# Attention scores in 16 array tiles of 32x32, the second token tile reversed, a new order of all calls

## The chip, the cores and the metric

The kernel runs on one core of a Trainium2 chip. A core has five engines with queues of their own: TensorE (PE) for matrix products, VectorE (DVE), ScalarE (ACT), GpSimd (POOL), and SyncE (SP), which issues most DMAs. They meet only through semaphores. The time is that of one execution on the device in microseconds; lower is better. Everything is fp32 but two mask constants.

## The reference, cut to what matters

For 8 batches of 256 tokens of 128 features, with xn = layernorm(x), the kernel adds three things: x, a one-head attention block with an output norm (a0/h0 in the names), and a transformer block with 16 heads of 8 features and causal attention, followed by a gated sum over four small expert networks. The part that the change touches:

```python
h = _rms(x, n1_w)
heads = lambda w_: (h @ w_.T).reshape(B, T, HEADS, HD).transpose(0, 2, 1, 3)
q = _rms(heads(wq), qn_w); k = _rms(heads(wk), kn_w); v = heads(wv)
scores = jnp.einsum('bhqd,bhkd->bhqk', q, k) * HD ** (-0.5)
scores = jnp.where(causal[None, None], scores, -jnp.inf)
attn = jax.nn.softmax(scores, axis=-1)
ao = jnp.einsum('bhqk,bhkd->bhqd', attn, v)...@ wo.T
```

The experts are: e0 = gelu, down; e1 = silu gate, product, down; e2 = four layers with three gelus (l1, l2, l3, down); e3 = two gelus (in, up, down). The gate is a softmax over four logits of which the two largest are kept.

## The kernel before, in words

A batch is two token tiles of 128 (j for queries, kt for keys). Every engine has a hand-written list of small functions, called with the batch number (`batches()` on PE and VectorE, straight lists on GpSimd and ScalarE); the order of the calls is the schedule, and work of several batches is interleaved in it. PSUM is eight banks: four hold one group of scores (`scores_ps`), the other four (a, b, even, odd) are handed from use to use by `claim`, which waits until the reader of the last use is done.

The heads are taken in 4 groups (g) of 4 lanes. A lane is a strip of 32 rows of the PE array: `qT` has the transposed queries of all heads, `kT[:, g]` the keys in which all features but those of the group's heads are zero, so that 32 rows of both, multiplied, give one head's scores. `scores(n, g)` (L229) puts keys on the partitions and queries on the columns: for key tile 0 all 256 queries, for key tile 1 the last 128 only, since earlier queries don't see them. That is 2 x 4 products, each in an array tile of 32 rows x 128 columns (L246). `exp_group` (L724) takes the exponential of all 4 x 384 columns at once, `mask` (L563) on GpSimd zeroes the later keys in the two diagonal 128x128 squares of each lane with one select, `weigh_v` (L271, L275) multiplies by the values and, through a column of ones in `v_aug`, sums the weights; VectorE transposes and divides (`pv_turn`, `heads_inverse`, `heads_divide`, `ao_turn`), PE projects (`wo_project`), and the residual, its norm and the transposed `xfT` feed the experts (`up_layer` L333, `square_layer` L360, `e3_up_layer` L376, `down` L392).

Ahead of the scores stand, for each batch: `ln_statistics` (VectorE), `ln_variance`, `ln_pow` (GpSimd), `ln_normalise`, `x_turn` (PE transposes xn, L186), `qkv_project` (L216), `qkv_copy` (ScalarE), `qk_square` to `qk_norm` on VectorE (a reciprocal root by a guess and corrections), `qk_turn` (PE, L186), `q_copy` and `k_copy` (ScalarE). `fold_weights` multiplies two weight matrices once.

The softmax takes no maximum if a bound on the weights allows it. VectorE computes that flag at run time (`bound_scores`), each of PE and VectorE reads it and takes one of two branches. With the inputs used here the branch without maximum runs (`searching = False`).

Of the kernel before, what the change touches and what calls it, by code (L numbers as in the profile page):

```python
# [4 lines left out]
ALU = mybir.AluOpType  # L5
# [6 lines left out]
P = 128  # L12
# [18 lines left out]
def fused_block(nc: bass.Bass, x, cols, rows, w_proj, w_first, w_up, w_mid, w_down, out):  # L31
# [5 lines left out]
    TILES = SEQ // P  # L37
# [9 lines left out]
    with ExitStack() as ctx:  # L47
# [9 lines left out]
        def sem(name):  # L57
# [30 lines left out]
        minus_half = sb("minus_half", [P, TILES])  # L88
        lower = sb("lower", [P, EXPERTS, EXPERTS])
# [50 lines left out]
        names = """ident_ready lower_ready lanes_ready cols_in rows_in flags_in proj_in first_in up_in mid_in down_in  # L140
                   proj_scaled m0_full m0_ready vfc_full vfc_ready flag_ready k_rows_ready zeros_ready masks_ready
# [28 lines left out]
        def _(pe):  # L170
# [58 lines left out]
            def scores(n, g):  # L229
# [10 lines left out]
                if n == 0 and g == 0:  # L240
                    pe.wait_ge(s["vfc_ready"], 1)
                for kt in range(TILES):
                    for lane in range(LANES):
                        rows = slice(32 * lane, 32 * lane + 32)
                        ps = scores_ps[:, lane, 0:SEQ] if kt == 0 else scores_ps[:, lane, SEQ:SEQ + P]
                        ins = T.matmul(ps, kT[p][rows, g, kt * P:(kt + 1) * P], qT[p][rows, kt * P:SEQ],  # L246
                                       start=kt == 0, stop=kt == 1 and not searching, tile_position=(32 * lane, 0))
                if searching:
# [6 lines left out]
                    for lane in range(LANES):  # L255
                        own = scores_ps[:, lane, :].rearrange("p (n q) -> p n q", q=SEQ)[:, :, 0:P]
                        ins = T.matmul(own, ident_bf[:], later_keys[:].unsqueeze(1).to_broadcast([P, TILES, P]),
                                       start=False, stop=True)
# [138 lines left out]
            def find_maxima(n):  # L397
# [11 lines left out]
                for r, (j, kt) in enumerate(ROUND_LIST):  # L409
# [8 lines left out]
                    if kt == j:  # L418
                        for lane in range(LANES):
                            ins = T.matmul(scores_ps[:, lane, :].rearrange("p (g k) -> p g k", k=P), ident_bf[:],  # L420
                                           later_keys_q[:].unsqueeze(1).to_broadcast([P, GROUPS, P]), start=False,
                                           stop=True)
# [8 lines left out]
            def batches():  # L431
                x_turn(0); qkv_project(0, 0); fold_weights(); q0_project(0); qkv_project(0, 1); a0_scores(0, 0)
                a0_scores(0, 1); x_turn(1); qk_turn(0); q0_project(1); find_maxima(0); scores(0, 0); x_turn(2)
                qkv_project(1, 0); scores(0, 1); qkv_project(1, 1); fc_row(0); scores(0, 2); a0_scores(1, 0)
                weigh_v(0, 0); weigh_v(0, 1); scores(0, 3); a0_scores(1, 1); weigh_v(0, 2); x_turn(3); weigh_v(0, 3)
                fc_row(1); qk_turn(1); q0_project(2); find_maxima(1); scores(1, 0); wo_project(0); qkv_project(2, 0)
                a0_scores(2, 0); scores(1, 1); qkv_project(2, 1); a0_scores(2, 1); scores(1, 2); weigh_v(1, 0)
                xf_turn(0); weigh_v(1, 1); scores(1, 3); gate(0); l1_layer(0); e3_in(0); weigh_v(1, 2); x_turn(4)
                weigh_v(1, 3); e1_first(0); e3_up_layer(0); qk_turn(2); wo_project(1); l2_layer(0); e0_up(0)
                fc_row(2); find_maxima(2); scores(2, 0); l3_layer(0); e1_second(0); xf_turn(1); qkv_project(3, 0)  # L440
                scores(2, 1); e3_in(1); gate(1); down(0, 0); down(0, 1); q0_project(3); scores(2, 2)
                qkv_project(3, 1); e3_up_layer(1); l1_layer(1); scores(2, 3); weigh_v(2, 0); weigh_v(2, 1)
                l2_layer(1); e0_up(1); weigh_v(2, 2); weigh_v(2, 3); e1_first(1); qk_turn(3); e1_second(1)
                wo_project(2); find_maxima(3); scores(3, 0); l3_layer(1); a0_scores(3, 0); qkv_project(4, 0)
                scores(3, 1); xf_turn(2); qkv_project(4, 1); down(1, 0); gate(2); down(1, 1); x_turn(5); scores(3, 2)
                e1_first(2); e0_up(2); scores(3, 3); weigh_v(3, 0); l1_layer(2); e1_second(2); q0_project(4)
                weigh_v(3, 1); e3_in(2); a0_scores(3, 1); weigh_v(3, 2); weigh_v(3, 3); l2_layer(2); e3_up_layer(2)
                wo_project(3); qk_turn(4); fc_row(3); l3_layer(2); a0_scores(4, 0); find_maxima(4); scores(4, 0)
                qkv_project(5, 0); down(2, 0); down(2, 1); xf_turn(3); qkv_project(5, 1); scores(4, 1); l1_layer(3)
                e0_up(3); gate(3); scores(4, 2); weigh_v(4, 0); l2_layer(3); e3_in(3); a0_scores(4, 1); weigh_v(4, 1)  # L450
                scores(4, 3); weigh_v(4, 2); l3_layer(3); e3_up_layer(3); fc_row(4); weigh_v(4, 3); x_turn(6)
# [945 lines left out]
```

## Time and profile before

| what | us |
|---|---|
| median of 3 runs | 233.01 (232.93 to 233.16) |
| profiled execution | 233.21 |
| its span in the profile | 231.5 |
| PE busy | 199.3 |
| ScalarE busy | 170.2 |
| VectorE busy | 153.4 |
| GpSimd busy | 107.7 |

The busy times are unions of an engine's instructions over the span. PE's instructions overlap each other, and the ends of its instructions are modelled by the profiler; the distance between two starts is the surer measure. `PEld` is PE's loading of the fixed operand, which runs beside the products. The granted clock is the share of PE's full 2.4 GHz that the chip let through: 1.00 or 0.50.

### The profile page before, as it was taken

The numbers are of one execution on the slowest core, as the hardware profiler recorded it, in microseconds if no ns is written. First come the engines' busy times: TensorE is split into PE (matmuls) and PEld (weight loads), VectorE is DVE, ScalarE is ACT, GpSimd is POOL, SyncE is SP. The second block draws the span as 40 slices with busy tenths as digits, with TensorE's granted clock in tenths as the row PEclk, the third lists the DMA queues.
The fourth block names the chain that finished last, engine by engine and source line by source line (L and its number), as shares of the span: only waits on it lengthen the run. The fifth ranks groups of instructions, "written<-read, shape, count | busy, mean of one in ns | idle before, by whom it ended". The sixth has DMA issues, their size and how long they took to land. (4 is left out here: it accounts for less than half of the span.)

```text
span 231.5 us, 5985 instructions
## 1 busy us (share of the span) xinstructions
PE 199.3 (86%) x2132; PEld 145.4 (63%) x2132; DVE 153.4 (66%) x534; ACT 170.2 (74%) x288; POOL 107.7 (47%) x190
## 2 busy tenths in 40 slices
PE   0557765989999998898999899999999999969892
PEld 0325433656868765765777678667786786747682
DVE  6453489279837881597669486797479847843354
ACT  2225843778998989997989998899999677636610
POOL 6851587865381715251476266515622536720000
PEclk9985999599999999999999999999999999999999
DMA  5930000000000000000000000000000000000001
GB/s 130 385 97 1 4 0 0 3 1 3 0 1 3 25 0 0 3 25 1 1 3 27 0 0 3 27 0 4 0 25 0 4 0 25 3 0 0 1 3 52
DMA packets 5393, 5.00 MB, mean 22 GB/s; under 512 B 498, under 2 KB 4850, under 8 KB 5362
## 3 DMA queue, kind: packets, MB, share of 16 engines
q1 hardware_dynamic: 5072, 4.39, 5.8%
q8 instruction: 19, 0.31, 0.5%
q10 hardware_dynamic: 290, 0.20, 0.4%
q14 instruction: 12, 0.10, 0.1%
HBM read 3.54 MB, written 1.05 MB: 20 GB/s over the span
## 5 line engine op out<-in xcount | busy, mean ns | idle before, releaser
L563 POOL TENSOR_SCALAR_AFFINE_SELECT probs<-probs 128x1024 f32<-128x1024 f32 x32 | 35.3, 1102 | 49.2 <-ACT probs L724 48.9
L724 ACT ACTIVATE probs<-scores_ps 128x1536 f32<-128x1536 f32 x32 | 46.4, 1449 | 6.9 <-PE scores_ps L246 6.6
L246 PEld LDWEIGHTS scores_ps<-qT,kT 32*128 32x128 f32 x512 | 24.8, 195 | 15.4 <-issue 11.8
L246 PE MATMUL scores_ps<-qT,kT 32*128 32x128 f32 (+1 forms) x512 | 31.7, 363 | 3.1 <-ACT probs L724 3.0
L360 PE MATMUL even_ps<-l_h,mid 128*128 128x256 f32 x128 | 31.8, 391 | 1.1 <-DVE e_s L1029 1.1
L360 PEld LDWEIGHTS even_ps<-l_h,mid 128*128 128x128 f32 x128 | 23.0, 189 | 6.8 <-DVE e_s L1029 1.7
L778 ACT ACT_TABLE_LOAD x18 | 23.1, 1283 | 2.3 <-PE even_ps L360 1.8
L333 PE MATMUL odd_ps<-xfT,up 128*128 128x256 f32 x80 | 21.8, 387 | 0.2 <-DVE e_h L1040 0.2
L271 PE MATMUL a_ps<-probs,v_aug 128*32 128x256 f32 x256 | 20.3, 389 | 1.5 <-DVE pv_rows L1048 1.4
L778 ACT ACTIVATE l_h<-even_ps 128x512 f32<-128x512 f32 x24 | 14.4, 599 | 8.7 <-PE even_ps L360 6.8
L1235 DVE SCALAR_TENSOR_TENSOR acc<-even_ps,wts,acc 128x96 f32<-128x96 f32 x32 | 10.2, 318 | 14.2 <-PE even_ps L392 11.7
L333 PE MATMUL even_ps<-xfT,up 128*128 128x256 f32 x64 | 17.8, 400 | 0.4 <-DVE e_s L1029 0.2
L333 PEld LDWEIGHTS odd_ps<-xfT,up 128*128 128x128 f32 x80 | 14.5, 190 | 3.1 <-DVE e_h L1040 0.8
L216 PE MATMUL a_ps<-qkvT,xnT 128*128 128x384 f32 x32 | 15.2, 558 | 0.6 <-ACT xnT L742 0.6
L284 PE MATMUL b_ps<-xnT,q0T 128*128 128x256 f32 x32 | 11.2, 435 | 4.0 <-ACT a_exp L731 4.0
L731 ACT ACTIVATE a_exp<-b_ps,a_negmax 128x256 f32<-128x256 f32 x16 | 7.5, 472 | 9.1 <-DVE a_negmax L1122 9.1
L830 ACT ACTIVATE kT<-a_ps,k_rows 128x256 f32<-128x256 f32 x32 | 13.7, 493 | 0.0
L186 PE MATMUL b_ps<-ident,xn 128*128 128x128 f32 x16 | 4.0, 336 | 11.0 <-DVE xn L1222 8.1
L333 PEld LDWEIGHTS even_ps<-xfT,up 128*128 128x128 f32 x64 | 11.0, 189 | 3.4 <-ACT l_h L778 1.3
L724 ACT ACT_TABLE_LOAD x10 | 12.8, 1283 | 0.2
L275 PE MATMUL a_ps<-probs,v_aug 128*32 128x128 f32 x256 | 12.9, 273 | 0.0
L1048 DVE STREAM_TRANSPOSE pv_rows<-a_ps 128x512 f32<-128x512 f32 x16 | 11.3, 704 | 1.8 <-PE a_ps L275 1.8
(149 smaller groups left out, 433.3 us busy)
## 6 DMA issues: line engine op xcount, KB each, us to landing
x_sb<-in_x SPq DMA_DIRECT2D x8, 128.0 KB, 6.5
out<-acc SPq DMA_DIRECT2D x8, 128.0 KB, 1.8
mid<-in_mid SPq DMA_DIRECT2D x1, 640.0 KB, 7.4
up<-in_up SPq DMA_DIRECT2D x1, 578.0 KB, 6.3
downs<-in_down SPq DMA_DIRECT2D x1, 512.0 KB, 8.2
first<-in_first SPq DMA_DIRECT2D x1, 320.0 KB, 5.6
proj<-in_proj SPq DMA_DIRECT2D x1, 192.0 KB, 2.9
row<-in_rows ACTq DMA_DIRECT2D x1, 192.0 KB, 4.8
```

The lines of the kernel that those rows point to most:

```text
L216: T.matmul(ps[:, 0:3 * D], xnT[n % X_COPIES][:, j * P:(j + 1) * P], qkvT[:], start=True, stop=True).then_inc(full_sem(fill), 1)
L246: ins = T.matmul(ps, kT[p][rows, g, kt * P:(kt + 1) * P], qT[p][rows, kt * P:SEQ], start=kt == 0, stop=kt == 1 and not searching, tile_pos ...
L271: T.matmul(rows, v_aug[p][:, 0, GROUPS * lane + g, :], probs[g][:, lane, 0:SEQ], start=True, stop=False, tile_position=(0, 32 * lane))
L275: ins = T.matmul(rows[:, P:SEQ], v_aug[p][:, 1, GROUPS * lane + g, :], probs[g][:, lane, SEQ:SEQ + P], start=False, stop=True, tile_positi ...
L284: T.matmul(ps, q0T[n % Q0_COPIES][:, j * P:(j + 1) * P], xnT[n % X_COPIES][:], start=True, stop=True).then_inc(full_sem(fill), 1)
L333: ins = T.matmul(ps[:, m * SEQ:(m + 1) * SEQ], wT[:, m * P:(m + 1) * P], xfT[n % XF_COPIES][:], start=True, stop=True)
L360: ins = T.matmul(ps[:, m * SEQ:(m + 1) * SEQ], wT[:, at_col:at_col + P], src[:, ci, :], start=(ci == 0), stop=(ci == HC - 1))
L563: nc.gpsimd.affine_select(out=own, in_=own, compare_op=ALU.is_ge, fill=0.0, base=0, pattern=[[0, LANES * TILES], [1, P]], channel_multipli ...
L724: nc.scalar.activation(probs[g][:, :, 0:SEQ + P], scores_ps[:, :, 0:SEQ + P], ACT.Exp).then_inc(s["exp_done"], 1)
L778: nc.scalar.activation(dst[n % 2][:].rearrange("p c q -> p (c q)"), ps_of(fill), ACT.Gelu).then_inc(read_sem(fill), 1)
L830: nc.scalar.activation(kT[n % HEAD_COPIES][:, g, :], ps_of("QKT")[:, SEQ:2 * SEQ], ACT.Copy, scale=k_rows[:, g:g + 1]).then_inc(s["k_copie ...
L1048: V.transpose(pv_rows[n % 2][:, 2 * pair:2 * pair + 2].rearrange("p g n e -> p (g n e)"), ps_of(fill)).then_inc(read_sem(fill), 1)
```

## The change

- `scores`: all groups but the first of batch 0 are now 32 products in array tiles of 32 rows x 32 columns: for each key tile, 4 blocks of 32 keys x 4 lanes. A block of key tile 0 takes only the queries from its own first key on (256, 224, 192, 160 columns).
- The second token tile is stored in reverse, on the host, on the way in and out. In it a block of keys c is seen by the first 32c + 32 stored queries (32, 64, 96, 128 columns). What the skipped places of PSUM hold from before goes through the exponential and is zeroed by the mask.
- `mask`: two selects of 128x512, one for each token tile, with opposite comparisons, in place of one of 128x1024.
- The branch with a maximum keeps whole products and gets a second mask constant.
- `v_aug` is filled with ones by ScalarE (three `fill_heads`) in place of three pairs of memsets on VectorE.
- `keep_busy(count)`: products of a zeroed tile into the bank "odd" that nobody reads, 3 ahead of the flag's read and 10 in the first calls of batch 0.
- The rows' constants (bias, gamma, beta) are loaded by SP's queue after x(2), not by ScalarE's; x(4) is loaded ahead of `mid`.
- All four lists of calls are new.

```diff
+            def keep_busy(count):
+                for _ in range(count):
+                    T.matmul(banks["odd"][:, 0:SEQ], spare[:, 0:P], spare[:], start=True, stop=True)
...
+                whole = searching or (n == 0 and g == 0)
                 for kt in range(TILES):
-                    for lane in range(LANES):
-                        rows = slice(32 * lane, 32 * lane + 32)
-                        ps = scores_ps[:, lane, 0:SEQ] if kt == 0 else scores_ps[:, lane, SEQ:SEQ + P]
-                        ins = T.matmul(ps, kT[p][rows, g, kt * P:(kt + 1) * P], qT[p][rows, kt * P:SEQ],
-                                       start=kt == 0, stop=kt == 1 and not searching, tile_position=(32 * lane, 0))
+                    if whole:
...
+                        continue
+                    for c in range(P // 32):
+                        keys = slice(kt * P + 32 * c, kt * P + 32 * c + 32)
+                        at_col, seen = (32 * c, slice(32 * c, SEQ)) if kt == 0 else (SEQ, slice(P, P + 32 * c + 32))
+                        for lane in range(LANES):
+                            rows = slice(32 * lane, 32 * lane + 32)
+                            ins = T.matmul(scores_ps[32 * c:32 * c + 32, lane, at_col:at_col + seen.stop - seen.start],
+                                           kT[p][rows, g, keys], qT[p][rows, seen], start=kt == 0, stop=kt == 1,
+                                           tile_position=(32 * lane, 32 * c))
...
             def mask(n, g):
                 pool.wait_ge(s["exp_done"], GROUPS * n + g + 1)
-                own = probs[g][:].rearrange("p l (n q) -> p (l n) q", q=SEQ)[:, :, 0:P]
-                nc.gpsimd.affine_select(out=own, in_=own, compare_op=ALU.is_ge, fill=0.0, base=0,
-                                        pattern=[[0, LANES * TILES], [1, P]], channel_multiplier=-1
-                                        ).then_inc(s["masked"], 1)
+                for kt, sign in enumerate((1, -1)):
+                    own = probs[g][:, :, kt * SEQ:kt * SEQ + P]
+                    ins = nc.gpsimd.affine_select(out=own, in_=own, compare_op=ALU.is_ge, fill=0.0, base=0,
+                                                  pattern=[[0, LANES], [sign, P]], channel_multiplier=-sign)
+                ins.then_inc(s["masked"], 1)
...
+            def fill_heads(p):
+                if p == 0:
+                    act.wait_ge(s["halves_ready"], 1)
+                nc.scalar.activation(v_aug[p][:].rearrange("p j h e -> p (j h e)"),
+                                     minus_half[:, 0:1].to_broadcast([P, TILES * HEADS * 32]), ACT.Copy, scale=-2.0
+                                     ).then_inc(s["heads_filled"], 1)
```

The first calls of PE's new list, and its last (before, the first scores had two of batch 1's calls ahead of them, `x_turn(1)` and `q0_project(1)`, and the list ended in `down(6, 0); down(6, 1); down(7, 0); down(7, 1)`):

```diff
+                keep_busy(4); fold_weights(); x_turn(0); keep_busy(1); qkv_project(0, 0); x_turn(1); qkv_project(0, 1)
+                q0_project(0); qkv_project(1, 0); a0_scores(0, 0); qkv_project(1, 1); keep_busy(3); x_turn(2)
+                keep_busy(1); q0_project(1); qkv_project(2, 0); a0_scores(0, 1); qk_turn(0); fc_row(0); find_maxima(0)
+                scores(0, 0); a0_scores(1, 0); qkv_project(2, 1); scores(0, 1); a0_scores(1, 1); qk_turn(1)
+                scores(0, 2); x_turn(3); keep_busy(1); scores(0, 3); weigh_v(0, 0); weigh_v(0, 1); fc_row(1)
...
+                xf_turn(7); l3_layer(6); e3_in(7); gate(7); down(6, 0); down(6, 1); a0_scores(7, 1); e1_first(7)
+                e3_up_layer(7); fc_row(7); l1_layer(7); e1_second(7); l2_layer(7); e0_up(7); l3_layer(7); down(7, 0)
+                down(7, 1)
```

## Rows read from the trace of the kernel before

**Rows 1.** The page, busy time, share and instructions of TensorE

```profile
PE 199.3 (86%) x2132; PEld 145.4 (63%) x2132; DVE 153.4 (66%) x534; ACT 170.2 (74%) x288; POOL 107.7 (47%) x190
```

**Rows 2.** Windows: stretch, its length, busy us of each engine, clock, DMA

```profile
core 0: us, PE busy (x) PEld busy (x) DVE busy (x) ACT busy (x) POOL busy (x), PEclk, DMA share, GB/s
15.60:22.40 6.80, 4.50 (x18) 2.69 (x22) 3.82 (x19) 2.78 (x10) 2.15 (x6) 0.50 0.00 1
30.90:39.50 8.60, 4.06 (x47) 2.35 (x44) 8.46 (x24) 3.03 (x8) 7.17 (x12) 1.00 0.00 0
39.50:46.30 6.80, 6.76 (x42) 4.09 (x45) 2.68 (x10) 5.30 (x14) 5.16 (x9) 0.50 0.01 2
60.00:180.00 120.00, 115.65 (x1292) 86.34 (x1294) 85.48 (x304) 110.78 (x177) 56.23 (x87) 1.00 0.03 7
200.00:220.00 20.00, 16.54 (x90) 12.40 (x82) 9.48 (x35) 10.28 (x21) 3.22 (x6) 1.00 0.00 0
```

**Rows 3.** Timeline of PE, one group cut at 120.30, then whole: start, us, what

```profile
120.26 0.50 PE L246 MATMUL scores_ps<-qT,kT 32*128 32x256 f32 x4
...
120.26 0.94 PE L246 MATMUL scores_ps<-qT,kT 32*128 32x256 f32 x16
121.12 1.13 PE L333 MATMUL even_ps<-xfT,up 128*128 128x256 f32 x4
```

**Rows 4.** Timeline of PE, the gate's small products

```profile
123.05 0.40 PE L321 MATMUL b_ps<-up,xfT 128*64 128x4 f32 x8
```

**Rows 5.** Timeline of PE, values in four tiles of 32 columns

```profile
124.24 0.64 PE L271 MATMUL a_ps<-probs,v_aug 128*32 128x256 f32 x8
```

**Rows 6.** Timeline of the first 11 us, several engines; in brackets idle before, releaser

```profile
4.87 0.14 DVE L913 TENSOR_SCALAR bounded<-widest 1x1 int32<-1x1 f32 x1
5.87 0.19 POOL L648 TENSOR_SCALAR ln_tmp<-ln_mv 128x2 f32<-128x2 f32 x1 [0.40 <-DVE ln_mv L1215]
7.55 0.69 PE L186 MATMUL b_ps<-ident,xn 128*128 128x128 f32 x2 [7.55 <-DVE xn L1222]
8.80 1.65 PE L216 MATMUL a_ps<-qkvT,xnT 128*128 128x384 f32 x2 [0.56 <-ACT xnT L742]
10.24 0.63 PE L191 MATMUL scores_ps<-first 128*128 128x128 f32 x2
```

**Rows 7.** Timeline from 19 to 41 us, PE and VectorE

```profile
19.53 1.09 PE L186 MATMUL a_ps<-ident,qk_n 128*128 128x128 f32 x4
21.46 1.40 PE L246 MATMUL scores_ps<-qT,kT 32*128 32x256 f32 x16
26.56 0.61 DVE L1140 SCALAR_TENSOR_TENSOR h<-b_ps,a_row,xn_b 128x128 f32<-128x128 f32 x2 [6.90 <-PE b_ps L293]
38.72 0.66 PE L186 MATMUL a_ps<-ident,qk_n 128*128 128x128 f32 x4 [1.66 <-DVE pv_rows L1048]
40.21 1.67 PE L246 MATMUL scores_ps<-qT,kT 32*128 32x256 f32 x16
```

**Rows 8.** Timeline of ScalarE, an exponential, a tanh, a table load

```profile
214.11 0.21 ACT L774 ACTIVATE gate_b<-gate_a 128x8 f32<-128x8 f32 x1
214.23 0.58 ACT L767 ACTIVATE e_t<-even_ps 128x512 f32<-128x512 f32 x1
214.82 1.28 ACT L778 ACT_TABLE_LOAD   x1
```

**Rows 9.** Groups of GpSimd by line: count, busy us, mean ns, idle before

```profile
L563 POOL TENSOR_SCALAR_AFFINE_SELECT probs<-probs 128x1024 f32<-128x1024 f32 x32 | 35.3, 1102 | 49.2 <-ACT probs L724 48.9
L529 POOL TENSOR_SCALAR_AFFINE_SELECT ident<-ident 128x128 f32<-128x128 f32 x1 | 0.3, 298 | 0.2 <-POOL ident L528 0.2
```

**Rows 10.** Timeline of PE at the end

```profile
218.41 1.96 PE L360 MATMUL even_ps<-l_h,mid 128*128 128x256 f32 x8
220.21 1.03 PE L333 MATMUL odd_ps<-xfT,up 128*128 128x256 f32 x4
221.17 0.88 PE L392 MATMUL even_ps<-downs,e_h 128*64 128x96 f32 x16
224.26 0.88 PE L392 MATMUL even_ps<-downs,e_h 128*64 128x96 f32 x16 [0.23 <-DVE acc L1235]
```

More of the change, by code:

```diff
@@ L431, in batches @@
             def batches():
[L432 to L451, printed above, removed]
@@ new lines, in batches @@
+                scores(1, 1); wo_project(0); qkv_project(3, 1); a0_scores(2, 0); scores(1, 2); weigh_v(1, 0)
+                weigh_v(1, 1); a0_scores(2, 1); scores(1, 3); xf_turn(0); weigh_v(1, 2); l1_layer(0); gate(0)
+                e3_in(0); x_turn(4); weigh_v(1, 3); l2_layer(0); qk_turn(2); e3_up_layer(0); wo_project(1)
+                e1_first(0); e0_up(0); fc_row(2); find_maxima(2); scores(2, 0); e1_second(0); l3_layer(0); xf_turn(1)
+                qk_turn(3); scores(2, 1); gate(1); e3_in(1); q0_project(3); down(0, 0); down(0, 1); scores(2, 2)
@@ new lines, in batches @@
+                qkv_project(4, 1); x_turn(5); l3_layer(2); wo_project(3); e3_up_layer(2); qkv_project(5, 0)
+                q0_project(4); down(2, 0); xf_turn(3); qkv_project(5, 1); e3_in(3); l1_layer(3); e0_up(3); l2_layer(3)
+                gate(3); down(2, 1); a0_scores(4, 0); e1_first(3); qk_turn(4); e1_second(3); x_turn(6); find_maxima(4)
+                scores(4, 0); e3_up_layer(3); l3_layer(3); scores(4, 1); qk_turn(5); down(3, 0); down(3, 1)
+                scores(4, 2); weigh_v(4, 0); weigh_v(4, 1); scores(4, 3); a0_scores(4, 1); weigh_v(4, 2); fc_row(4)
@@ new lines, in batches @@
+                weigh_v(4, 3); find_maxima(5); scores(5, 0); q0_project(5); qkv_project(6, 0); scores(5, 1)
+                wo_project(4); qkv_project(6, 1); a0_scores(5, 0); scores(5, 2); weigh_v(5, 0); a0_scores(5, 1)
+                scores(5, 3); xf_turn(4); weigh_v(5, 1); e3_in(4); l1_layer(4); gate(4); weigh_v(5, 2); fc_row(5)
+                e0_up(4); l2_layer(4); x_turn(7); weigh_v(5, 3); e3_up_layer(4); qk_turn(6); l3_layer(4)
+                find_maxima(6); scores(6, 0); wo_project(5); e1_first(4); e1_second(4); q0_project(6)
@@ L468, in _ @@
+            keep_busy(3)
             pe.wait_ge(s["flag_ready"], 1)
@@ L706, in _ @@
+            h0_add(7); x1_add(7)
         @block.scalar
@@ L1341, in _ @@
+                down(7, 1, 2); down(7, 1, 3)
+            V.memset(spare[:], 0.0).then_inc(s["spare_ready"], 1)
             bound_scores()
```

321 lines of the change are left out of this document (161 added, 160 removed).

## Prediction, made before the change ran

> **What bounds the kernel now.** I read the page's shares first: TensorE (PE) leads with 86% of the span [rows 1]. A share is an average over stages, so next comes the table of windows [rows 2]. From 60 to 180 us PE is busy for 115.65 of 120 us and ScalarE for 110.78: there PE sets the pace with ScalarE close behind, and a us taken from PE alone is worth nearly a us only as long as ScalarE follows. The same table shows two stretches of 6.8 us, 15.6 to 22.4 and 39.5 to 46.3, in which the granted clock was 0.50 (1.2 of 2.4 GHz). The second was full of work, 6.76 us of it. Ahead of it, from 30.9 to 39.5, PE had 4.06 us of work in 8.6 us. So PE was starved, fell to half clock, and then paid double for its work. The sum is made against the profiled execution, 233.21 us with a span of 231.5; the median of the runs is 233.01, so what holds for the one holds for the other within 0.2.
>
> **Scores in 16 tiles.** One group of scores (L246) is 8 products, 16 matrix instructions: an fp32 product takes two. What it costs is not the 0.94 of its row but the distance to the next start, 120.26 to 121.12, 0.86 us [rows 3]. The price of a column: eight instructions of 256 columns (L360) from 218.41 to the next product at 220.21, 1.80 us [rows 10], 0.225 each, 0.88 ns a column. Each lane streams 256 + 128 = 384 columns twice: 0.675 us. The other 0.185 is the first weight load and the switch to other products. That lanes overlap is in the rows: four instructions have begun in the first 0.05 us, and sixteen one after the other would take over 2 us [rows 3]. Now each of 16 tiles streams 288 columns (256+32, 224+64, 192+96, 160+128): 2 x 288 x 0.88 = 0.507. If all sixteen overlap as the four do, a group is 0.507 + 0.185, and 0.05 for twelve more starts at the rate of those four: 0.74 us. 31 groups change (the first stays whole): 31 x 0.12 = -3.7. Bounds: 0.65 from below (no stagger, a shorter weight load), -6.5; from above the nearest row of small products is L321, eight instructions of 4 columns in 0.40, 0.05 us each [rows 4]; 64 such are 3.2 us, +73 in all. I stay near the scores' own row: L321 has two tiles at a time, while the four starts within 0.05 us show that the stream of instructions is faster.
>
> **The clock and the hole before it.** The new order projects batch 1 ahead of the first scores and puts qk_turn(1) before scores(0, 2). Before, qk_turn(1) was the product at 38.72 that waited for VectorE, busy 8.46 of those 8.6 us, and scores(1, 0) could only follow at 40.21 [rows 2, 7]. VectorE had stood idle for 6.9 us until 26.56 [rows 7]; its work for batch 1 can go there. Of 4.5 us of idle PE I take 3.0 as filled (bounds 0 and 4.5). With that the fall of the clock at 39.5 has lost its cause: half of 6.76, -3.4 (bounds 0 and -3.4).
>
> **The head.** Idle products (two instructions of 256 columns, 0.45 us at full clock, twice that at half) raise the clock earlier. Batch 0's chain had at half clock a transpose of 0.69, a projection of 1.65, four transposes of 1.09 and the first scores, 1.40 [rows 6, 7], 4.83 together. The scores' row is 0.94 at full clock, a third less [rows 3]; a third to a half of 4.83 is 1.6 to 2.4: -2.0. The weight products and what they wait for (10.24 until the next projection step, 1.1) leave the middle of the chain: -1.1. Against it x_turn(0) now stands behind four idle products, which start when the flag is there (4.87 + 0.14) and last 3.6 at half clock, and behind four short weight instructions: about 9.2 instead of 7.55, +1.6. Net -1.5, bounds +2 and -3. The memsets leave VectorE, but GpSimd took up batch 0's variance at 5.87 after only 0.40 of waiting [rows 6], its constants stay ahead of it, so at most 0.4 comes of that, counted as nothing; on ScalarE the three fills (1024 elements, 1.1 us each by the 0.58 for 512 [rows 8]) lie before its first copy, which waits for the product at 7.55. Should the fills last until 9 they would delay it by what is over. The shift of the rows' DMA to SP's queue puts it behind three loads and puts x(3) and the three large weight loads behind it; its reader (biased) is not on batch 0's chain: nothing. If it is late, h0_variance and masks behind it on GpSimd's queue are late too.
>
> **ScalarE.** Its list of functions changes kind (exponential against gelu) 34 times instead of 38, if tanh costs no switch on either side. The rows show that: tanh at 214.23 stands right behind an exponential at 214.11 with no load between, and the load comes for the gelu behind it [rows 8]. A load is 1.28 us: -5.1 of ScalarE's work. In 60 to 180 PE idles only 4.35 us, so a quarter of it, -1.3, is taken (0 to -3).
>
> **The masks.** One select over 1024 elements is 1.10 us, one over 128 is 0.30 [rows 9]. On that line 512 cost 0.64, two 1.29: +0.19 a group, +6 for GpSimd, which has room. On the path only in the last batch: +0.2.
>
> **The tail.** Before, four down calls stood at the end, batch 6's from 221.17, batch 7's from 224.26 [rows 10]. Now the two of batch 6 go before batch 7's expert layers, into 3.46 us of idle PE between 200 and 220 [rows 2]: -3.1. Late next is the last gelu (0.58 for 512 elements by tanh's row [rows 8]), once covered by e1_second at 220.21: +0.7. a0_scores(7, *) and fc_row(7) move behind scores(7, 3), four instructions of 256 columns and two short ones: +1.1. Net -1.3, bounds -3 and +1.
>
> Searching branch, masks in it and the flipping of x and out on the host: not executed on the chip in this run, nothing. The sum: -3.7 -3.0 -3.4 -1.5 -1.3 +0.2 -1.3 = -14.0, and +0.5 for waits that a wholly new order brings and that I can't see (0 to +5): 233.2 - 13.5 = 219.7 us.
>
> **A rule against it.** The rows show four lanes in the array at once although each product comes as two instructions of one lane [rows 3]. The Trainium skill ("TensorE: Matmul & The Clock Gate", Part 3, on what overlaps) says that matmuls start and end strictly in the order of the program. By it a block of keys would hold up the next one; what that costs is the first rival, worked out there from rows. The Trainium skill ("TensorEngine Tiling (Array Packing)", Instruction Overhead) also warns of some 60 cycles a matmul and of splitting a dimension that is already small; here the shortest are 32 columns. By 60 cycles, 25 ns at full clock, an estimate from that page, 64 instructions are 1.6 us a group and the change loses; its case in rows is in rival 3.
>
> **Rival 1, slower: blocks wait for each other.** The second instruction of a tile waits for its first, and the next block's first may not start before it. Then the blocks run as a staircase: 256 columns, 256 beside 224, 224 beside 192, 192 beside 160, which is 928; then, with the last 160 beside the second key tile's first blocks, 32 + 64 + 96 + 128 + 128 = 448. 1376 columns of 0.88 ns are 1.21, with 0.185 a group of 1.40 instead of 0.86: 31 x 0.54 = +16.7. In place of -3.7 this gives 240.1. The point from which it decides: all other terms save 9.8, which 31 groups eat at +0.32 each, a group of 1.18 us. For it: four concurrent instructions are all that any row shows. Against it: within four tiles the instructions already step past each other.
>
> **Rival 2: the order doesn't fill the hole.** Then the clock falls again and the head gains nothing: only scores, loads, masks and tail, 233.2 - 3.7 - 1.3 + 0.2 - 1.3 = 227.1. For it: VectorE is busy 8.46 of 8.6 us in that hole, its work is not less, and GpSimd's is more. Against it: its idle time before 26.56.
>
> **Rival 3: tiles of one row strip don't overlap at all.** 4 x 0.507 + 0.185 = 2.21 a group, +1.35 x 31 = +42: 265. A floor of 0.03 us an instruction, under L321's 0.05 [rows 4], would cost nearly as much and is in this case. For it: nothing but that no row shows rows and columns split at once; against it: rows alone (L246) and columns alone (L271, eight instructions of 256 columns in 0.64 us, where eight in a row take 1.80 [rows 5, 10]) both overlap.
>
> **Chances.** Forecast 0.62 (own range 213 to 227), rival 1 0.14, rival 2 0.14, rival 3 0.05, an order that stalls by over 10 us for another reason 0.05 (about 235). Faster by over 0.2%, which is about what a measurement can tell here: 0.62 + 0.14 and 0.02 of the edges of rival 1, 0.78. Within 0.2%: 0.02. Slower: 0.20. The range of 212 to 238 leaves out rival 3, over half of rival 1 and the far edges of the rest, somewhat under 2 in 10.
>
> **What would show it.** Scores groups 0.7 to 0.8 us from start to next start, more than four instructions begun in the first 0.1 us (rival 1: four, and about 1.4; rival 3: over 2). Clock 1.0 from some 9 us on, no stretch of 0.50 before the end; scores(1, 0) near 30 rather than 40.21. 34 table loads. Two selects of 0.64 a group. From 60 to 180 PE still over 95% busy; if ScalarE has passed it, the scores' term is lost. Two down calls, not four, behind the last gelu. Wrong is the prediction if groups take over 0.9 us or PE has holes of several us beyond 12.

## The result, and the profile after

| | before | after |
|---|---|---|
| median | 233.03 us (232.93 to 233.16) | 230.68 us (230.6 to 231.09) |
| ratio | 1 | 0.9903, 95% interval 0.9885 to 0.992 |
| profiled span | 231.5 us | 229.3 us |

The forecast was 219.7. The kernel is 2.35 us faster, not 13.3: the direction held, the size did not. From the page of the kernel after, its busy line and the granted clock in 40 slices:

```profile
PE 211.5 (92%) x3646; PEld 150.9 (66%) x3646; DVE 137.4 (60%) x529; ACT 168.2 (73%) x287; POOL 110.8 (48%) x222
PEclk9999999999999999999999999999999999999998
```

TensorE has 12.2 us more work than in [rows 1], in a shorter span, and the clock no longer falls before the end. 5.7 of the 12.2 are the idle products (without them PE is busy for 205.8 us, below). So the clock and the hole were mended, and something in PE's own work got dearer. The page's groups name it (count, then busy us and mean ns, then idle before and its releaser):

```profile
L586 POOL TENSOR_SCALAR_AFFINE_SELECT probs<-probs 128x512 f32<-128x512 f32 x64 | 39.6, 643 | 50.9 <-ACT probs L754 50.9
L754 ACT ACTIVATE probs<-scores_ps 128x1536 f32<-128x1536 f32 x32 | 46.4, 1450 | 19.9 <-PE scores_ps L262 19.7
L262 PE MATMUL scores_ps<-qT,kT 32*32 32x256 f32 (+2 forms) x1984 | 40.0, 292 | 2.7 <-ACT probs L754 2.6
```

The second line is ScalarE's exponential. It waited 19.7 us in all for scores; in the kernel before the same group waited 6.6, and in the kernel with the new order but whole products (below) 12.7, so about half of the growth comes of the scores' tiles. The third line is the new scores, 31 groups of them in 40.0 us.

One group of scores in the timeline of TensorE, cut at six moments. Each line is the same group as far as a window reaches that ends at 78.82, 79.00, 79.34, 79.36, 79.50 and behind it; the last number is how many matrix instructions have begun:

```profile
78.71 0.42 PE L262 MATMUL scores_ps<-qT,kT 32*32 32x256 f32 x16
78.71 0.64 PE L262 MATMUL scores_ps<-qT,kT 32*32 32x256 f32 x32
78.71 0.65 PE L262 MATMUL scores_ps<-qT,kT 32*32 32x256 f32 x33
78.71 0.83 PE L262 MATMUL scores_ps<-qT,kT 32*32 32x256 f32 x34
78.71 1.05 PE L262 MATMUL scores_ps<-qT,kT 32*32 32x256 f32 x47
78.71 1.28 PE L262 MATMUL scores_ps<-qT,kT 32*32 32x256 f32 x64
79.92 0.55 PE L319 MATMUL b_ps<-first,aoT 128*64 128x96 f32 x8
```

All sixteen tiles have begun after 0.11 us, and the second instruction of each runs after 0.29: key tile 0 does just what was forecast. Then almost nothing begins for 0.34 us, from 79.00 to 79.34: a single instruction, the seventeenth product's first, at 0.46 us from the group's start. The thirty-fourth instruction begins at 0.644, the eighteenth product at 0.653, and from there products come one by one, the last at 0.886 (14 gaps of 16.7 ns, where the first sixteen were 6.7 ns apart). The next work starts 1.21 us after the group's start, where [rows 3] has 0.86. The other groups take the same (median 1.21; a few also wait for another engine). So 31 groups cost 31 x 0.348 = 10.8 us more of PE, not 3.7 less.

The windows of the kernel after over three of the stretches of [rows 2], with the same columns:

```profile
30.90:39.50 8.60, 7.82 (x194) 4.79 (x186) 6.82 (x23) 4.35 (x6) 6.28 (x14) 1.00 0.02 5
60.00:180.00 120.00, 116.85 (x2191) 83.71 (x2191) 71.87 (x270) 96.56 (x158) 53.01 (x93) 1.00 0.03 8
200.00:220.00 20.00, 18.46 (x143) 14.43 (x143) 11.03 (x50) 10.63 (x22) 4.65 (x8) 1.00 0.03 8
```

The hole of 30.9 to 39.5 is filled (7.82 of 8.6 us against 4.06). In 60 to 180 ScalarE's work has fallen by 14.2 us, to 96.56: it had been close behind PE and now trails it. Slower scores explain at most 4.2 of that, since the new order with whole products has 100.81 in the same stretch; the rest came with the order, which has fewer table loads and puts other calls into the stretch.

### The profile page after: what moved, and what is told of

The parts are those of the page before. It is cut to its first block, busy times and chain, and to the rows that moved or that the text cites. A ratio compares the mean times of both kernels' runs of the same rounds, so it can differ in the third digit from the quotient of the medians.

```text
span 229.3 us, 9039 instructions
## 1 busy us (share of the span) xinstructions
PE 211.5 (92%) x3646; PEld 150.9 (66%) x3646; DVE 137.4 (60%) x529; ACT 168.2 (73%) x287; POOL 110.8 (48%) x222
## 4 chain that ended last, share of the span: by engine, by line
PE 59%; POOL 12%; ACT 10%; issue 10%; DVE 7%; POOLq 0%; ACTq 0%; DVEq 0%
PE scores_ps L262 12%; PE even_ps L377 10%; PE odd_ps L350 6%; ACT probs L754 5%; PE even_ps L350 5%; PE even_ps L409 5%; PE a_ps L288 4%; PE odd_ps L409 4%; PE odd_ps L393 3%; POOL probs L586 3%; PE a_ps L222 2%; DVE acc L1259 2%; PE a_ps L292 2%; PE a_ps L187 1%; POOL ln_rstd L678 1%
## 5 line engine op out<-in xcount | busy, mean ns | idle before, releaser
L586 POOL TENSOR_SCALAR_AFFINE_SELECT probs<-probs 128x512 f32<-128x512 f32 x64 | 39.6, 643 | 50.9 <-ACT probs L754 50.9
L754 ACT ACTIVATE probs<-scores_ps 128x1536 f32<-128x1536 f32 x32 | 46.4, 1450 | 19.9 <-PE scores_ps L262 19.7
L262 PE MATMUL scores_ps<-qT,kT 32*32 32x256 f32 (+2 forms) x1984 | 40.0, 292 | 2.7 <-ACT probs L754 2.6
L262 PEld LDWEIGHTS scores_ps<-qT,kT 32*32 32x32 f32 x1984 | 25.5, 103 | 17.4 <-issue 9.8
L377 PE MATMUL even_ps<-l_h,mid 128*128 128x256 f32 x128 | 30.8, 383 | 0.2 <-DVE e_s L1053 0.2
L377 PEld LDWEIGHTS even_ps<-l_h,mid 128*128 128x128 f32 x128 | 23.7, 190 | 4.7 <-ACT l_h L808 0.9
L1259 DVE SCALAR_TENSOR_TENSOR acc<-even_ps,wts,acc 128x96 f32<-128x96 f32 x32 | 10.1, 317 | 18.3 <-issue 10.2
L808 ACT ACTIVATE l_h<-even_ps 128x512 f32<-128x512 f32 x24 | 14.3, 597 | 9.1 <-PE even_ps L377 8.3
L222 PE MATMUL a_ps<-qkvT,xnT 128*128 128x384 f32 x32 | 13.7, 509 | 1.2 <-ACT qkv L790 1.0
L1146 DVE TENSOR_REDUCE a_negmax<-b_ps 128x1 f32<-128x256 f32 x16 | 6.7, 417 | 9.4 <-PE b_ps L301 9.3
L790 ACT ACTIVATE qkv<-a_ps,h_scale 128x384 f32<-128x384 f32 x16 | 9.3, 580 | 3.8 <-PE a_ps L222 2.7
L292 PEld LDWEIGHTS a_ps<-probs,v_aug 128*32 128x32 f32 x256 | 8.4, 110 | 5.4
L1259 DVE SCALAR_TENSOR_TENSOR acc<-odd_ps,wts,acc 128x96 f32<-128x96 f32 x32 | 10.1, 316 | 1.3 <-PE odd_ps L409 0.5
```

Source lines behind the costliest of these rows:

```text
L222: T.matmul(ps[:, 0:3 * D], xnT[n % X_COPIES][:, j * P:(j + 1) * P], qkvT[:], start=True, stop=True).then_inc(full_sem(fill), 1)
L262: ins = T.matmul(scores_ps[32 * c:32 * c + 32, lane, at_col:at_col + seen.stop - seen.start], kT[p][rows, g, keys], qT[p][rows, seen], sta ...
L292: ins = T.matmul(rows[:, P:SEQ], v_aug[p][:, 1, GROUPS * lane + g, :], probs[g][:, lane, SEQ:SEQ + P], start=False, stop=True, tile_positi ...
L377: ins = T.matmul(ps[:, m * SEQ:(m + 1) * SEQ], wT[:, at_col:at_col + P], src[:, ci, :], start=(ci == 0), stop=(ci == HC - 1))
L586: ins = nc.gpsimd.affine_select(out=own, in_=own, compare_op=ALU.is_ge, fill=0.0, base=0, pattern=[[0, LANES], [sign, P]], channel_multipl ...
L754: nc.scalar.activation(probs[g][:, :, 0:SEQ + P], scores_ps[:, :, 0:SEQ + P], ACT.Exp).then_inc(s["exp_done"], 1)
```

## The experiments

All kernels below are the kernel after with one edit, unless it is said otherwise. They ran in three series on three chips: whole, 8 tiles (first runs), the old order and no idle products in one; key tile 1 whole, short first, no short and two blocks in the next; bf16 and the repeats in the last. The kernel before took 233.78, 233.34 and 233.81 us there. Their expectations speak of a theory A and rivals where each defines them; the later ones of a queue theory, spelled out there.

| kernel | what a group of scores is | start to next start | median us | ratio to before, 95% |
|---|---|---|---|---|
| after, again | 32 products of 32x32 | 1.21 | 230.82 (6 runs) | 0.9868 [0.982, 0.9916] |
| no short | 32 products, none under 128 columns | 1.21 | 230.48 (1 run) | |
| key tile 1 whole | 16 of 32x32, 4 of 32x128 | 1.10 | 227.84 | 0.973 [0.9648, 0.9812] |
| short first | 32 of 32x32, key tile 1 first | 0.93 | 226.2 | 0.9656 [0.9574, 0.9737] |
| whole | 8 of 32x128 | 0.86 | 223.9 | 0.9576 [0.9495, 0.9658] |
| 8 tiles of 32x64 | 16 of 32x64 | 0.73 | 223.86; again 223.2 | 0.9529 [0.9441, 0.9617]; 0.9537 [0.9488, 0.9587] |
| two blocks | 16 of 32x32, half the keys' blocks | 0.65 | 222.12 (1 run) | |
| bf16 | 32 of 32x32, half as many instructions | 0.30 (0.47 in the group shown) | 222.09 | 0.9491 [0.943, 0.9552] |

**Whole products.** What is the rest of the change worth without the sixteen tiles?

```diff
-                whole = searching or (n == 0 and g == 0)
+                whole = True
```

> The changed kernel with all scores as whole products (8 of 32 rows x 128 columns a group, as before the change), all else as changed: reversed tile, two masks, new order. Theory A (the group's price): a 16-tile group takes 1.21 us from start to start instead of 0.86 and lies on PE's path, so 31 x 0.35 = 10.8 come off 230.7: 219.9, between 218.5 and 222, and groups of 0.86. Rival B (slack): another engine holds the new order, and less than half of it comes off: 226 to 230.

Measured: 223.9 us, 6.8 below the kernel after, with PE's busy time 201.2 us instead of 211.5. The sixteen tiles take 6.8 us of the run, 63% of the 10.8 that they cost PE; the rest is swallowed by waits. That lies between theory A (218.5 to 222) and rival B (226 to 230): neither holds whole. The scores now start at, in the timeline of this kernel:

```profile
33.42 0.94 PE L254 MATMUL scores_ps<-qT,kT 32*128 32x256 f32 x16
185.51 0.94 PE L254 MATMUL scores_ps<-qT,kT 32*128 32x256 f32 x16
```

These are scores(1, 0) and scores(7, 3). Everything but the scores' tiles brings 9.1 us against the kernel before of the result (233.0 to 223.9), 9.9 against that of its own series (233.78); the forecast said 9.8 for it. So the failed step lies in the scores.

**Sixteen tiles in the old order.** The kernel before with the new scores, the two masks and the reversed tile, its lists of calls kept:

```diff
-                    for lane in range(LANES):
...
+                    for c in range(P // 32):
...
+                for kt, sign in enumerate((1, -1)):
```

> The kernel before, its own order and all else, with only the scores in 16 tiles, the reversed second tile and the two masks. Theory A (group's price on PE's path): 31 x 0.35 = 10.8 more: 243.8, at least 241. Rival B (slack): 235 to 238. If the clock falls less, since PE is busier, up to 2 less than A says.

Measured: 237.67 us against 233.78 in the same series, ratio 1.0152 [1.0062, 1.0242]: alone, the sixteen tiles are a loss. The loss is 3.9 us, 36% of the 10.8 that PE pays, as rival B had it, so the old order absorbs more of it than the new one does (PE was busy 86% of the span there [rows 1], 91% in the kernel with whole products). Part of that is the clock: it is at 0.50 from 17.9 to 24.7 and from 35.0 to 38.4 us here, 10.2 us in all against 13.6 in [rows 2], which by my estimate, half of the difference, gives back up to 1.7 us. Its page:

```profile
PE 208.7 (88%) x3620; PEld 147.5 (62%) x3620; DVE 149.6 (63%) x534; ACT 170.2 (72%) x288; POOL 113.1 (48%) x222
PEclk9995997999999999999999999999999999999999
```

**Eight tiles of 32x64.** The same idea with half as many products:

```diff
-                    for c in range(P // 32):
-                        keys = slice(kt * P + 32 * c, kt * P + 32 * c + 32)
+                    for c in range(P // 64):
+                        keys = slice(kt * P + 64 * c, kt * P + 64 * c + 64)
```

> The changed kernel with scores in 8 array tiles of 32 x 64 (blocks of 64 keys: 256 and 192 columns for key tile 0, 64 and 128 for key tile 1), 32 instructions a group instead of 64. Theory A (each tile runs by itself as long as a group's instructions fit the queue): 2 x 320 columns x 0.88 ns + 0.185 = 0.75 a group, 31 x 0.46 = 14.3 off 230.7: 216.4. Rival C (halves wait for the longest tile of the round): second instructions of all tiles start together, a round lasts as long as its widest tile, 256+256+128+128 columns, 0.86 a group: 219.9, no better than whole products.

Measured: 223.86 us (222.44 to 225.15). The timeline of one group:

```profile
78.21 0.80 PE L262 MATMUL scores_ps<-qT,kT 32*64 32x256 f32 x32
78.94 0.55 PE L319 MATMUL b_ps<-first,aoT 128*64 128x96 f32 x8
```

A group takes 0.73 us, the figure that I had forecast for sixteen tiles, and by the same formula: 2 x 320 columns x 0.88 + 0.185 = 0.75. So halves of a product don't wait for the longest tile (rival C). But scores that are 31 x 0.13 = 4.1 us shorter than whole ones brought at most 1.5 (the two runs with a clock of 0.999 took 222.44 and 222.74), and nothing in the median. Below about 0.86 a group most of PE's time isn't what the run waits for, and in half of these runs the clock fell as well (0.984 and 0.985: 225.15 and 224.98).

**No idle products.** The kernel after without the thirteen:

```diff
             def keep_busy(count):
-                for _ in range(count):
+                for _ in range(0):
```

> The changed kernel without the 13 idle products. Theory D (they hold the clock up in the head): a stretch of 0.50 comes back in the first 25 us, and the time grows by 1.5 to 3 us. Rival E (the new order alone keeps PE busy enough, and the four idle products ahead of x_turn(0) delay it): no change or up to 1 us less.

Measured: 232.54 us, 1.9 above the kernel after. The head of this kernel, and below it that of the kernel after:

```profile
7.57 0.64 PE L187 MATMUL b_ps<-ident,xn 128*128 128x128 f32 x2
8.77 1.65 PE L222 MATMUL a_ps<-qkvT,xnT 128*128 128x384 f32 x2 [0.56 <-ACT xnT L772]
```

```profile
4.39 2.17 PE L192 MATMUL odd_ps<-spare 128*128 128x256 f32 x7
6.43 0.49 PE L197 MATMUL scores_ps<-first 128*128 128x128 f32 x2
7.38 0.44 PE L187 MATMUL b_ps<-ident,xn 128*128 128x128 f32 x2 [0.23 <-DVE xn L1246]
8.38 0.91 PE L222 MATMUL a_ps<-qkvT,xnT 128*128 128x384 f32 x2
```

The projection takes 1.65 us at half clock and 0.91 behind idle products (half clock is read from these lengths: the profile's record of the clock begins only at 12.5 us in this kernel, at 5.4 in the kernel after). The first scores start at 21.86 without them and at 20.36 with them.

**None short.** Now the pause itself. Two causes were open: the short products (32 columns), or the number of instructions. First the length, with the number kept:

```diff
-                        at_col, seen = (32 * c, slice(32 * c, SEQ)) if kt == 0 else (SEQ, slice(P, P + 32 * c + 32))
+                        at_col, seen = (32 * c, slice(32 * c, SEQ)) if kt == 0 else (SEQ, slice(P, SEQ))
```

> After with all 128 columns for every block of key tile 1, so 16 tiles and 64 instructions' worth of products as before, but none shorter than 128 columns. In the kernel after, a group of scores starts its first instructions 6.7 ns apart, the second key tile's first product at 0.459 us, then pauses 0.185 us and goes on with one product every 16.7 ns; 1.213 us to the next start. Queue theory (TensorE holds about 64 instructions with their weight loads, key tile 0 fills it, the rest are brought in late): pause and 16.7 ns stay, group 1.2 to 1.3. Short-product theory (the 32-column products block the stream): no pause, group 0.85 to 0.95.

Measured: a group of 1.21 us, unchanged, and 230.48 us. In its timeline, cut at 79.30 and whole:

```profile
78.70 0.72 PE L262 MATMUL scores_ps<-qT,kT 32*32 32x256 f32 x33
78.70 1.28 PE L262 MATMUL scores_ps<-qT,kT 32*32 32x256 f32 x64
79.91 0.55 PE L319 MATMUL b_ps<-first,aoT 128*64 128x96 f32 x8
```

The same 33 instructions have begun before the pause. A group now streams 192 more columns per lane, 384 with both instructions, and takes no longer: behind the pause it isn't columns that cost. The theory of short products is out.

**Two blocks.** Then the number, with the short ones kept. This kernel leaves out blocks 2 and 3 of the keys in both key tiles:

```diff
-                    for c in range(P // 32):
+                    for c in range(2):
```

> After with blocks 0 and 1 only, in both key tiles: half of the keys' blocks are left out, a group has 16 products, 64 instructions with weight loads, and the shortest products (32 and 64 columns) stay. Queue theory: all 64 fit, no pause, the second key tile's products start within 0.05 us of each other, group 0.60 to 0.75. Short-product theory: the pause of 0.185 us behind the first 32-column product stays, and 16.7 ns a product after it, group 0.85 to 1.0.

Measured: 0.65 us a group. In its timeline, cut at 76.90, 76.98, 77.00 and whole:

```profile
76.50 0.63 PE L262 MATMUL scores_ps<-qT,kT 32*32 32x256 f32 x16
76.50 0.66 PE L262 MATMUL scores_ps<-qT,kT 32*32 32x256 f32 x24
76.50 0.71 PE L262 MATMUL scores_ps<-qT,kT 32*32 32x256 f32 x30
76.50 0.72 PE L262 MATMUL scores_ps<-qT,kT 32*32 32x256 f32 x32
77.15 0.55 PE L319 MATMUL b_ps<-first,aoT 128*64 128x96 f32 x8
```

No pause: all eight products of key tile 1 begin within 0.05 us (0.430 to 0.476 from the group's start). Block 1, second in the program, even begins ahead of block 0: the first four of these records are 0.214 us long (64 columns), the next four 0.188 (32 columns). Such freedom needs the instructions to be at hand. With 64 of them (two weight loads and two matrix instructions a product) they are.

**Key tile 1 whole.** A dose in between: 16 + 4 products, 80 instructions.

```diff
-                    if whole:
+                    if whole or kt == 1:
```

> After with key tile 0 in 16 tiles and key tile 1 in its four whole products (32x128 tiles, 128 columns): 20 products, 80 instructions with weight loads, none short. Queue theory: key tile 0's 64 fill the queue, four products come late; pause of about 0.185 us stays, then 3 x 16.7 ns, then 2 x 128 columns: group 0.95 to 1.05, run time between that of the kernel after (230.7) and that of whole products (223.9), about 226 to 228. Short-product theory: no pause, 2 x 384 columns for the first block as in a whole group: 0.86 to 0.90 and 223.9 to 225.

Measured: 1.10 us a group and 227.84 us. The pause is there with no short product in sight, so the count decides again; both my figures were too low for the group. The first whole product began only at 0.567 us, against 0.46 for the small one; it needs all four tiles of its row strip and a load of 128 columns, which would explain that, but no run separates the two:

```profile
77.99 0.64 PE L262 MATMUL scores_ps<-qT,kT 32*32 32x256 f32 x32
78.56 0.60 PE L254 MATMUL scores_ps<-qT,kT 32*128 32x128 f32 x8
79.09 0.55 PE L319 MATMUL b_ps<-first,aoT 128*64 128x96 f32 x8
```

**Short ones first.** The same 128 instructions in another order:

```diff
-                for kt in range(TILES):
+                for kt in (range(TILES) if whole else (1, 0)):
```

> After with key tile 1 (32 to 128 columns) ahead of key tile 0 in each group, nothing else. Queue theory: the short ones fill the queue's 64 and are through sooner, so the pause lies beside less work but is still there, and key tile 0's products come one each 16.7 ns after it; last start near 0.6, 2 x 160 columns behind it: group 0.95 to 1.1, run time 225 to 229. Short-product theory: the stream stalls behind the first short product from the start, 16.7 ns a product for 31 of them: group 1.2 to 1.4, run time 230 to 234.

Measured: 0.93 us a group, just under the lowest figure expected, 0.95, and 226.2 us. The group cut at 78.69 and 78.73, then whole:

```profile
78.44 0.61 PE L262 MATMUL scores_ps<-qT,kT 32*32 32x32 f32 x33
78.44 0.68 PE L262 MATMUL scores_ps<-qT,kT 32*32 32x32 f32 x34
78.44 1.00 PE L262 MATMUL scores_ps<-qT,kT 32*32 32x32 f32 x64
79.37 0.55 PE L319 MATMUL b_ps<-first,aoT 128*64 128x96 f32 x8
```

Again 33 instructions and then a gap, but a short one: the thirty-fourth begins at 0.278 instead of 0.644. Where it begins follows from the first product. The record of that product's second instruction ends at 0.244 here (begun at 0.053, 32 columns, 0.191 long) and at 0.617 in the kernel after (begun at 0.243, 256 columns, 0.374 long); the thirty-fourth comes 0.034 and 0.027 us later. Without short products the pair is 0.615 and 0.643, with key tile 1 whole 0.617 and 0.654: 0.028 and 0.037 later. So the reading that fits all four: a place comes free when the oldest product is done. The gain of this order follows from it, since the oldest is then a short one.

**Half as many instructions, as many products.** Are the 64 instructions, or sixteen open products? Queries and keys in bf16 take one weight load and one matrix instruction a product:

```diff
-        qT, negT = sbs("qT", HEAD_COPIES, [P, SEQ]), sbs("negT", HEAD_COPIES, [P, SEQ])
-        kT = sbs("kT", HEAD_COPIES, [P, GROUPS, SEQ])
+        qT, negT = sbs("qT", HEAD_COPIES, [P, SEQ], BF16), sbs("negT", HEAD_COPIES, [P, SEQ])
+        kT = sbs("kT", HEAD_COPIES, [P, GROUPS, SEQ], BF16)
```

> After with queries and keys stored in bf16, so that a product of scores is one weight load and one matrix instruction instead of two of each; 32 products a group are then 64 instructions, not 128. The numbers of the scores are coarser. Instruction-queue theory (64 instructions with loads fit): no pause at all, all 32 products begin within 32 x 8.4 ns or as soon as their tile is free, group 0.40 to 0.55, run time 218 to 223. Rival, the limit is 16 or 17 open products, whatever they consist of: the pause behind the seventeenth product stays, at a time that its shorter streams set, group 0.60 to 0.75.

Measured: all 32 products have begun 0.131 us after the first. Cut at 78.30 and at 78.38:

```profile
78.23 0.29 PE L262 MATMUL scores_ps<-qT,kT 32*32 32x256 bf16 x16
78.23 0.34 PE L262 MATMUL scores_ps<-qT,kT 32*32 32x256 bf16 x32
78.70 0.55 PE L319 MATMUL b_ps<-first,aoT 128*64 128x96 f32 x8
```

The next work starts 0.47 us after this group. In ten of the 31 groups it starts after 0.30, with all products begun after 0.13 just the same, so the longer distance is no price of the scores. One of the ten:

```profile
81.75 0.34 PE L262 MATMUL scores_ps<-qT,kT 32*32 32x256 bf16 x32
82.06 0.67 PE L288 MATMUL a_ps<-probs,v_aug 128*32 128x256 f32 x8
```

The run took 222.09 us, but its clock was at half from 21.2 to 34.8 and from 140.7 to 144.1 us of the profiled run, so this time doesn't show what such short groups are worth.

No pause with 32 products, so the limit is in instructions. It fits 64 with weight loads counted. 32 matrix instructions alone would fit as well, and no run here separates the two. Either way the places come free in order. In the kernel after, the seventeenth product's first load and first matrix instruction, the 65th and 66th of the burst, begin at 0.244 and 0.459 us, when the first load and the first matrix instruction have ended (0.101 and 0.402).

**Filling the thin stretch.** In its profiled run the kernel of eight tiles fell to half clock for some 3.4 us at 28.7. More idle products there:

```diff
-                scores(0, 2); x_turn(3); keep_busy(1); scores(0, 3); weigh_v(0, 0); ...
+                scores(0, 2); keep_busy(2); x_turn(3); keep_busy(2); scores(0, 3); weigh_v(0, 0); ...
```

> The version with 8 tiles of 32x64, with two idle products ahead of x_turn(3) and one more ahead of scores(0, 3), where TensorE waited for ScalarE for 1.07 and 0.56 us and the granted clock then fell for 3.4 us in its profiled run. If that fall came of the thin stretch at 24 to 29 us: no fall there, and a median nearer to the 222.4 and 222.7 of the undisturbed runs, 221.5 to 223, with a smaller spread. If the fall has nothing to do with it: spread and median as in the repeat, and up to 0.7 us more for idle products in the way.

> The version with 8 tiles of 32x64 once more, unchanged, beside the next one: 222.3 to 225.2, as in its first runs.

> The kernel after, unchanged, on the chip of the other three: 230.6 to 231.1, 7 to 8 us above 8 tiles of 32x64.

Measured on one chip: 223.78 us (222.5 to 224.24) with more idle products, 223.2 (222.58 to 224.97) without, 230.82 (230.66 to 230.97) for the kernel after. The windows of 27.2 to 30.6 and 139.4 to 142.8, with the columns of [rows 2], first eight tiles as first run, then with more idle products:

```profile
27.20:30.60 3.40, 2.65 (x44) 1.83 (x48) 0.38 (x3) 2.89 (x8) 3.15 (x6) 0.72 0.00 0
139.40:142.80 3.40, 2.08 (x42) 0.90 (x26) 1.71 (x5) 2.40 (x5) 3.40 (x6) 0.78 0.02 7
```

```profile
27.20:30.60 3.40, 3.26 (x63) 2.28 (x66) 0.37 (x3) 3.40 (x8) 3.15 (x6) 1.00 0.00 0
139.40:142.80 3.40, 3.33 (x22) 2.09 (x23) 1.20 (x6) 3.31 (x5) 2.84 (x6) 0.58 0.01 2
```

The first fall is gone, the second stays, and the median doesn't improve. Eight tiles of 32x64 are 7.6 us under the kernel after and 10.6 under before. They are not shown to beat whole products: 222.44 to 225.15 in one series, where whole products took 223.86 to 225.72.

## Why the prediction was wrong, step by step

**Scores: the step that failed.** The forecast was "If all sixteen overlap as the four do, a group is 0.507 + 0.185, and 0.05 for twelve more starts": 0.74 us, -3.7. The group took 1.21, and the term came out at +6.8. The sixteen do overlap, and so near the forecast that the seventeenth product, the next for the first tile, begins at 0.46. (One figure in the sum was small: twelve more starts at the rate of four in 0.05 us are 0.15, not 0.05; measured, at 6.7 ns each, 0.08.) What the sum lacked is supply. It added the second key tile's columns as if its instructions were at hand; they are not, past 64. The Trainium skill ("TensorE: Matmul & The Clock Gate", Part 1, on the array's 16 sub-arrays) gives TensorE's queue as 64 deep. The runs agree: 64 instructions pass without a pause in three kernels (eight tiles of fp32, two blocks, sixteen tiles of bf16), 80 and 128 do not. I counted 64 matrix instructions a group and never the 64 loads beside them, and set neither against any depth. All groups of scores in the kernel before are of 32 instructions, so its trace couldn't show the limit.

**The rivals.** By its own sign ("if groups take over 0.9 us") the forecast is wrong. Rival 1, the staircase at 1.40 us a group and 240.1, had the scores' sign right and the reason wrong: all four blocks begin at once. Its point of decision, "all other terms save 9.8, which 31 groups eat at +0.32 each", would have made the measured +0.348 slightly slower. It came out 2.35 us faster because of the 10.8 us only 6.8 reach the end. So the forecast's direction held by luck: its first term had the wrong sign and was outweighed by the others. Rival 3 is out, and rival 2 too.

**A us of PE is not a us.** This was assumed for the scores in full. The table of the experiments shows the slope: from 1.21 to 0.86 us a group 63% of the saving arrives on the whole (its steps are uneven: 3.0 of 3.4 us, 1.6 of 5.3, 2.3 of 2.2, across three chips), from 0.86 to 0.73 about a third at most. Below that little is shown: two blocks, 0.65 us a group, took 222.12 in a single run at full clock, and bf16 was slowed by its clock. So even a group of 0.74 wouldn't have given 219.7; the kernel that has 0.73 runs at 222.4 to 225. Who waits instead can be read from the chains of the kernel after, of whole products and of eight tiles (its first profiled run, in which the clock fell twice), shares of the span by engine:

```profile
PE 59%; POOL 12%; ACT 10%; issue 10%; DVE 7%; POOLq 0%; ACTq 0%; DVEq 0%
```

```profile
PE 45%; ACT 16%; issue 13%; POOL 12%; DVE 11%; POOLq 1%; ACTq 0%; DVEq 0%
```

```profile
PE 43%; ACT 19%; issue 13%; POOL 12%; DVE 11%; POOLq 1%; ACTq 0%; DVEq 0%
```

PE's share of the chain falls by 16 points, 14 of them already with whole products. ScalarE has 9 of the 16, VectorE 4, and 3 are time in which no wait is seen. By line, ScalarE's exponential went only from 5% to 6%; 3% are now table loads ahead of gelus (L808) and 2% those ahead of exponentials (L754), neither of which is among the fifteen lines that the page of the kernel after shows.

**The other terms,** by the starts of groups of scores in the timelines (us):

| stretch, from the one above it | before | whole products | difference | forecast |
|---|---|---|---|---|
| to scores(0, 0) | 21.46 | 20.35 | -1.1 | head -1.5 |
| to scores(1, 0) | 18.75 | 13.07 | -5.7 | hole -3.0, and part of the clock's -3.4 |
| to scores(2, 0) | 22.42 | 21.13 | -1.3 | rest of the clock |
| to scores(7, 3) | 132.96 | 130.96 | -2.0 | loads -1.3, masks, waits +0.5 |
| to the end | 35.9 | 36.7 | +0.8 | tail -1.3, masks +0.2 |

Hole and clock: forecast -6.4, measured -7.0 over both stretches, in which the order is also another. The head came close, for partly other reasons. I had x_turn(0) at "about 9.2"; it starts at 7.38. The flag's arithmetic, at 4.87 in [rows 6], now stands at:

```profile
2.41 0.14 DVE L937 TENSOR_SCALAR bounded<-widest 1x1 int32<-1x1 f32 x1
```

In the kernel before, the memsets of v_aug kept VectorE busy ahead of it until 4.45; I had "counted as nothing" that they leave. So the four idle products behind the flag began at 3.96 instead of 5.01, their instructions went from 0.43 to 0.22 us apart at 5.2, and the last of them began at 6.18. They delayed nothing that shows: without idle products the weight products behind them start at 6.55, when their DMA lands, and x_turn(0) at 7.57. The idle products are worth 1.5 us in the head by their own experiment, the forecast had 2.0. The selects take 643 ns, forecast 0.64. The table loads are 34, as forecast; two of their six groups:

```profile
L808 ACT ACT_TABLE_LOAD x16 | 20.5, 1283 | 1.1 <-PE even_ps L377 0.3 <-PE odd_ps L350 0.3 <-PE odd_ps L393 0.3
L754 ACT ACT_TABLE_LOAD x8 | 10.3, 1283 | 0.1
```

**The tail** was the other step that went wrong, by 1.9 us (+0.8 in a stretch for which -1.3 and +0.2 were forecast). Forecast: the down calls of batch 6 go "into 3.46 us of idle PE", -3.1. The windows from scores(7, 3) to the end, kernel before and whole products:

```profile
195.59:231.50 35.91, 27.85 (x279) 21.88 (x278) 18.90 (x67) 14.73 (x26) 6.82 (x10) 0.99 0.03 10
```

```profile
185.51:222.20 36.69, 29.54 (x288) 22.79 (x284) 18.04 (x74) 17.88 (x32) 7.68 (x13) 0.97 0.05 13
```

PE's idle time fell by 0.91 us only (8.06 to 7.15), and its work rose by 1.69. The calls left the end, but the last gelu had been covered by them: now batch 7's down calls wait 1.25 us for it, against 0.23 before them in [rows 10], and the moved a0_scores and fc_row are in the way as forecast. The line from the kernel after, where the wait is 1.24:

```profile
221.90 0.88 PE L409 MATMUL even_ps<-downs,e_h 128*64 128x96 f32 x16 [1.24 <-ACT l_h L808]
```

Idle time inside a stretch was taken as room that work could use; it is a chain of waits that stays when work is put beside it. Of this reading the windows show the sum, not each part: no run changed the tail alone.

Added up: scores +6.8 instead of -3.7 is 10.5 of the 11.0 us missed, and the rest of the change (-9.1 instead of -9.8) another 0.7, less the 0.2 by which the 233.2 that the sum started from lies above the median.

## What to carry to other kernels

Before splitting a product over more array tiles, count the instructions of a burst, weight loads included and doubled for fp32: here bursts of 64 ran without a pause, and with 80 and 128 the tiles waited for supply. If more can't be avoided, try the shortest products first; here that took 4.5 us off the run. And take a us saved on the leading engine at a us only as far as the next chain allows: here the slope was 0.63 down to a group of 0.86 us and about a third, at best, from there to 0.73.

## What the runs showed of the hardware

- A burst past 64 instructions: the thirty-fourth matrix instruction begins 0.027 to 0.037 us after the oldest product's record ends, and the rest at 16.7 ns a product of four instructions, 4.2 ns each. Within 64 products begin 6.7 ns apart in fp32 (four instructions) and 3.3 in bf16 (two), 1.7 ns an instruction in both.
- The order of starts isn't always the program's: with two blocks, the second key tile's block 1 begins at 0.430 us and its block 0, ahead of it in the program, at 0.456; with eight tiles the same blocks begin at 0.402 and 0.482. The Trainium skill ("TensorE: Matmul & The Clock Gate", Part 3, on what overlaps) says that matmuls start in order. Here the measurement decides, for products that take different tiles.
- 384 more columns per lane in a group cost nothing (1.21 and 1.21 us) once supply sets the pace.
- With shorter scores the clock fell again in some runs: with eight tiles it was 0.72 from 27.2 to 30.6 us and 0.78 from 139.4 to 142.8 in one run, and 0.999 on the mean in others of the same kernel. The bf16 kernel, with the least PE work (191.1 us), had the lowest mean clocks of the kernels in the new order, 0.961 to 0.984. It is no plain rule: two blocks, with 195.7 us of PE work, kept 1.000 in its one run.
